# Last layer of a two-layer gated block: the feed-forward's hidden values scaled one batch later, engines' orders rewritten, one reciprocal moved to VectorE

## The chip, the cores and the metric

One core of one Trainium2 chip runs the whole program. The time is the device time of one execution in microseconds (us), and the time shown for a kernel is the median of several executions. One execution was also recorded by the hardware profiler. TensorE is PE in the rows (its weight loads are PEld), VectorE is DVE, ScalarE is ACT, GpSimd is POOL, and SyncE (SP) issues the transfers.

## The reference

`x` and `ctx` are 32 batches of 256 tokens with 256 values each. Two layers are applied; the change touches only the last part of the second one.

```python
x = x + tanh(g_xattn[0]) * attention(layernorm(x), ctx, ctx)      # layer 0
x = x + tanh(g_ffn[0])   * L0_ffn(layernorm(x))
x = x + tanh(g_xattn[1]) * align(ctx, layernorm(x))   # layer 1: time warping of ctx to x
x = x + tanh(g_ffn[1])   * L1_ffn(layernorm(x))       # layer 1: feed-forward

def rmsnorm(x):    return x * rsqrt(mean(x * x, -1, keepdims=True) + 1e-5)
def act_quant(x):                                     # per token
    scale = 127 / clip(max(abs(x), -1), 1e-5)
    return clip(round(x * scale), -128, 127) / scale
def bitlinear(x, w, b):  return act_quant(rmsnorm(x)) @ weight_quant(w).T + b
def L1_ffn(x):                                        # 256 -> 1024 -> 256
    h = gelu(bitlinear(x, w1, b1), approximate=False)
    return bitlinear(h, w2, b2)
```

Each token's vector is thus rounded to integers twice: once at width 256 before the first product, and once at width 1024, after gelu, before the second. Both need the token's mean square and its largest absolute value first, and then a factor.

## The kernel before, in words

The program has three stages in a row. The attention stage (with layer 0's feed-forward) ends near 1250 us of the profile. The alignment stage ends near 1672 us. `last_layer_phase` takes the rest. The change lies in this last stage alone.

The last stage works on 32 batches `n`. A batch is two tiles (`t` = 0, 1) of 128 tokens on 128 partitions. For one batch the steps are: `distance` (ACT) and `path_mask` (DVE) build the alignment mask; `expand` (PE, tile `pe_x`) spreads ctx over the tokens; `residual` (DVE) adds it to x, giving `x3`; `stats`, `aggregate`, `centre`, `x_variance`, `x_maxima` (DVE) prepare the layer norm and the first rounding; `factors` (POOL) turns mean squares (`var`) and maxima (`amax`) into `y` = 1/rms, `q0` = 127/largest value, `q` = `q0*y`, and `back`, the factor for scaling back; `scale_x` (DVE, tile `xr`) and `round_x` (ACT, tile `xq`) round; `inverse_parts` (POOL) writes six columns with 1/`q0` in bf16 pieces behind `xq`; `turn_x` (PE, `pt_x`) transposes; `xqT_copy` (ACT) moves the result to SBUF; `hidden` (PE, `ph`, 12 matmuls) is the first product; `gelu` (ACT, `gl`); `squares` (ACT, `sq` and `ssum`) and `h_maxima` (DVE) prepare the second rounding; `factors` again; `scale_h` (DVE, `hr`) and `round_h` (POOL, `hq`) round; `turn_h` (PE, `pt_h`), `hqT_copy` (ACT) and `output` (PE, `po`, 16 matmuls) are the second product; `output` (DVE, `xo`) adds `x3b`, which `bias` (POOL) made from `x3`; SP stores.

The order is written by hand. Each engine has a loop over rounds `k`, from FIRST = -6 to LAST, and in round `k` it does each step for the batch `k` plus a fixed offset. So a batch passes through the stage over some nine rounds, and each engine meets many batches' steps in one round. Every engine runs its list strictly in order; `w(name, count)` is a wait on a semaphore. A step waits for its inputs, and also for its output buffer to be free: `pe_x`, `pt_x`, `pt_h`, `po`, `xr`, `xq`, `xqT` and `x3` exist once, `ph`, `hr` and `hqT` once for each tile `t`. `Chain` orders small dependent instructions on one engine: `link` waits for the instruction at once, `tick` only counts it, and `hold` waits for all counted so far.

`factors` on POOL handles batch `k+2`'s x and batch `k`'s hidden values together, in tensors of four columns, so that `scale_x(k+2)` and `scale_h(k)` follow on DVE in the same round `k`, behind `w("factors", ...)`.

Of the kernel before, what the change touches and what calls it, by code (L numbers as in the profile page):

```python
# [15 lines left out]
P = 128  # L16
# [1388 lines left out]
def last_layer_phase(nc, io, scr, vin, vout, out, o):  # L1405


    with ExitStack() as ctx:
# [3 lines left out]
        def sem(name):  # L1412
# [11 lines left out]
        x3b = [sb(f"x3b{p}", [P, T, D]) for p in range(6)]  # L1424
# [6 lines left out]
        y, tmp = sb("y4", [P, 2 * T]), sb("tmp4", [P, 2 * T])  # L1431
        back = [sb(f"back{p}", [P, 2 * T]) for p in range(4)]
        ws4, powers = sb("ws4", [P, 2 * T]), sb("powers", [P, 2, 2 * T])
        gl = [[sb(f"gl{p}{t}", [P, F]) for t in range(T)] for p in range(2)]
        sq = [sb(f"sq{t}", [P, F]) for t in range(T)]
        ssum = [sb(f"ssum{p}", [P, T]) for p in range(2)]
# [13 lines left out]
                 "ends", "masked", "x3_res", "x_scaled", "h_scaled", "x4_res", "x_max", "h_max", "factors",  # L1450
# [7 lines left out]
        FIRST, LAST = -6, NB + 2  # L1458
# [4 lines left out]
        @block.sync  # L1463
        def _(sp):
            def w(s, count):
                if count > 0:
                    sp.wait_ge(e[s], count)

            def load(n):
                w("expand", n - 2)  # L1470
                sp.dma_start(cx[n % 3][:], io["ctx_1024"][n].rearrange(tok, p=P)).then_inc(cx_in[n % 3], 16)
                w("x3_res", n - 2)
                sp.dma_start(x2[n % 3][:], scr["x2"][n].rearrange(tok, p=P)).then_inc(x2_in[n % 3], 16)

            def store(n):
                w("x4_res", n + 1)
                sp.dma_start(out[n].rearrange(tok, p=P), xo[n % 2][:]).then_inc(o_out[n % 2], 16)

            for k in range(FIRST, LAST):
                if there(k - 2):  # L1480
                    store(k - 2)
                if there(k + 6):
                    load(k + 6)
            for p in range(2):
                sp.wait_ge(o_out[p], 16 * NB // 2)

        @block.tensor
        def _(pe):
            def w(s, count):
                if count > 0:  # L1490
                    pe.wait_ge(e[s], count)

            def expand(n):
# [15 lines left out]
            def hidden(n):  # L1509
                w("xqT_cp", n + 1)  # L1510
                for t in range(T):
                    w("gelu", 2 * (n - 1) + t + 1)
                    for j in range(2):
                        for c in range(C + 1):
                            last = pe.matmul(ph[t][:, 512 * j:512 * j + 512], xqT[:, c, t * P:t * P + P],  # L1515
                                             w1T[:, c, 512 * j:512 * j + 512], start=(c == 0), stop=(c == C))
                    last.then_inc(e["h_mm"], 1)

            def turn_h(n, t):
                w("h_round", 2 * n + t + 1), w("hqT_cp", 2 * n + t)  # L1520
                for f in range(FT):
                    last = pe.transpose(pt_h[:, f, :], hq[n % 2][t][:, f * P:f * P + P], identb[:])  # L1522
                last.then_inc(e["hq_t"], 1)

            def output(n):
                w("x4_res", n)
                for t in range(T):
                    w("hqT_cp", 2 * n + t + 1)
                    for f in range(FT):
                        last = pe.matmul(po[:, t, :], hqT[t][:, f, :], w2T[:, f, :], start=(f == 0), stop=(f == FT - 1))  # L1530
                last.then_inc(e["o_mm"], 1)

            for k in range(FIRST, LAST):
                if there(k + 1):
                    hidden(k + 1)
                if there(k - 1):
                    turn_h(k - 1, 0)
                if there(k + 4):
                    expand(k + 4)
                if there(k - 1):  # L1540
                    turn_h(k - 1, 1)
                    output(k - 1)
                if there(k + 2):
                    turn_x(k + 2)

        @block.scalar
        def _(act):
# [4 lines left out]
            def gelu(n, t):  # L1552
                w("h_mm", 2 * n + t + 1), w("h_scaled", 2 * (n - 2) + t + 1)
                act.activation(gl[n % 2][t][:], ph[t][:], ACT.Gelu, scale=back[(n - 2) % 4][:, t:t + 1])\  # L1554
                    .then_inc(e["gelu"], 1)

            def squares(n, t):

                w("gelu", 2 * n + t + 1), w("squares", 2 * (n - 1) + t + 1)
                w("h_scaled", 2 * (n - 1))  # L1560
                act.activation(sq[t][:], gl[n % 2][t][:], ACT.Square, accum_out=ssum[n % 2][:, t:t + 1])\  # L1561
# [21 lines left out]
            for k in range(FIRST, LAST):  # L1583
                if there(k):
                    squares(k, 1)
                if there(k + 6):
                    distance(k + 6)
                if there(k - 1):
                    hqT_copy(k - 1, 0)
                if there(k + 1):  # L1590
                    gelu(k + 1, 0)
                if there(k - 1):
                    hqT_copy(k - 1, 1)
                if there(k + 1):
                    gelu(k + 1, 1)
                if there(k + 2):
                    round_x(k + 2)
                if there(k + 1):
                    squares(k + 1, 0)
                if there(k + 2):  # L1600
                    xqT_copy(k + 2)

        @block.gpsimd
        def _(pool):
# [6 lines left out]
            def bias(n):  # L1611
                w("x3_res", n + 1), w("x4_res", n - 5)
                for t in range(T):
                    last = pool.tensor_tensor(x3b[n % 6][:, t, :], x3[:, t, :], b2[:], ALU.add)  # L1614
                last.then_inc(e["x3_bias"], 1)

            def inverse_parts(n):

                w("xq_t", n)
# [13 lines left out]
            def factors(nx, nh):  # L1633
                p = nh % 2
                c = slice(0 if there(nx) else T, 2 * T if there(nh) else T)
                yy, aa = y[:, c], tmp[:, c]
                if there(nh):
                    w("squares", 2 * (nh + 1))
                    pc.link(pool.tensor_scalar(var[p][:, T:2 * T], ssum[p][:], 1.0 / F, EPS, ALU.mult, ALU.add))
# [3 lines left out]
                pc.link(pool.tensor_tensor(yy, var[p][:, c], powers[:, 0, c], ALU.pow))  # L1643
# [9 lines left out]
            pc.tick(pool.memset(powers[:, 0, :], -0.5))  # L1653
            pc.tick(pool.memset(powers[:, 1, :], -1.0))
# [15 lines left out]
        def _(v):  # L1670
# [41 lines left out]
            def h_maxima(n):  # L1712
                for t in range(T):
                    w("gelu", 2 * n + t + 1)
                    last = v.tensor_reduce(amax[n % 2][:, T + t:T + t + 1], gl[n % 2][t][:], AX.X, ALU.max,
# [3 lines left out]
            def output(n, t):  # L1719
                w("x3_bias", n + 1), w("o_mm", n + 1)  # L1720
                if n >= 2:
                    v.wait_ge(o_out[n % 2], 16 * (n // 2))
                ins = v.scalar_tensor_tensor(xo[n % 2][:, t, :], po[:, t, :], back[n % 4][:, T + t:T + t + 1],
                                             x3b[n % 6][:, t, :], ALU.mult, ALU.add)
# [9 lines left out]
            def scale_h(n):  # L1734
                for t in range(T):
                    w("h_round", 2 * (n - 1) + t + 1)
                    v.tensor_scalar(hr_[t][:], gl[n % 2][t][:], q[n % 2][:, T + t:T + t + 1], MAGIC, ALU.mult, ALU.add)\
                        .then_inc(e["h_scaled"], 1)

            def iteration(k):  # L1740
                nx, nh, nr, no, nm = k + 2, k, k + 3, k - 2, k + 5
                isx, ish, isr, iso, ism = (there(n) for n in (nx, nh, nr, no, nm))
                if ish:
                    h_maxima(nh)
                if isr:
                    residual(nr)
                if iso:
                    output(no, 0)
                    output(no, 1)
                if ism:  # L1750
                    path_mask(nm, 0)
                if isr:
                    stats(nr, 0)
                    stats(nr, 1)
                if ism:
                    path_mask(nm, 1)
                if isr:
                    aggregate(nr)
# [3 lines left out]
                    x_variance(nr)  # L1762
                    x_maxima(nr)
                if isx or ish:
                    w("factors", k + 3)
                if isx:
                    scale_x(nx)
                if ish:
                    scale_h(nh)
# [60 lines left out]
```

## Time and profile before

| | us |
|---|---|
| median of 3 executions | 2029.74 (2028.59 to 2030.02) |
| profiled execution | 2029.69 |
| its span | 2027.8 |

| busy in the span | PE | PEld | DVE | ACT | POOL |
|---|---|---|---|---|---|
| us | 1477.6 | 1064.4 | 1526.7 | 1089.5 | 608.0 |

The span covers the instructions of the execution; what lies around it is 1.9 us. The last stage begins at about 1672 us and ends with the span. In its rows an engine's instructions overlap a little: the next one starts some 0.1 us before the end of the one in front, so the time that an instruction holds its engine is read from one start to the next. `[1.18 <-POOL q L1650]` behind a row means that the engine had stood idle for 1.18 us before it, until POOL's instruction of line 1650 released it.

### The profile page before, as it was taken

The page shows a single profiled execution, that of the slowest core. Times are in us where ns is not written, and L with a number is a line of the kernel's source. Part 1 is how long each engine was busy: PE and PEld are TensorE (multiplying, and loading weights), DVE is VectorE, ACT ScalarE, POOL GpSimd, SP SyncE. Part 2 cuts the span into 40 slices and gives each one's busy share as a digit, 9 for nine tenths or more (in the row PEclk, how much of TensorE's full clock was granted, in tenths as well). Part 3 has the DMA queues.
Part 4 walks back from the last instruction along what each step waited for, and adds up shares of the span by engine and source line. Part 5 has one row for each costly group of instructions (what it writes and reads, how often), then busy time and mean ns, then how long its engine had stood idle before and what let it go on. Part 6 is the DMA issues. An engine that isn't in the chain of part 4 may idle for free. (4 is left out here: it accounts for less than half of the span.)

```text
span 2027.8 us, 35980 instructions
## 1 busy us (share of the span) xinstructions
PE 1477.6 (73%) x10790; PEld 1064.4 (52%) x10821; DVE 1526.7 (75%) x4466; ACT 1089.5 (54%) x2304; POOL 608.0 (30%) x1033
## 2 busy tenths in 40 slices
PE   1689999999999999999999986131331007777776
PEld 1467777777777777777777764000000004555554
DVE  7567777777776777777677743799998997888885
ACT  0266666666666666656666562242331005788876
POOL 3111222222222222222222111205000006888886
PEclk9799999999999999999999997555555557999999
DMA  2444443344444434444343310321220003222220
GB/s 79 121 121 132 118 128 111 108 125 112 133 117 115 120 108 129 112 133 113 109 123 105 107 38 18 90 58 39 60 45 7 0 0 99 79 71 78 79 67 32
DMA packets 322938, 179.51 MB, mean 89 GB/s; under 512 B 93793, under 2 KB 318193, under 8 KB 322802
## 3 DMA queue, kind: packets, MB, share of 16 engines
q1 hardware_dynamic: 322802, 178.07, 31.4%
q8 instruction: 40, 0.66, 0.1%
q14 instruction: 96, 0.79, 0.1%
HBM read 122.91 MB, written 50.33 MB: 85 GB/s over the span
## 5 line engine op out<-in xcount | busy, mean ns | idle before, releaser
L805 DVE TENSOR_REDUCE nmax<-s 128x2 f32<-128x512 f32 x512 | 325.4, 682 | 42.3 <-PE s L386 41.0
L601 ACT ACTIVATE pt<-s 128x512 f32<-128x512 f32 x512 | 277.3, 597 | 84.4 <-PE s L401 84.4
L892 POOL TENSOR_TENSOR r<-rl 128x512 f32<-128x512 f32 x128 | 133.1, 1040 | 372.6 <-ACT rl L631 370.0
L386 PE MATMUL s<-kst,qst 96*128 96x256 bf16 x1024 | 164.0, 276 | 19.4 <-DVE nmax L805 12.7
L401 PE MATMUL s<-qst,kst 128*128 128x256 bf16 x1024 | 168.0, 276 | 9.1 <-ACT pt L601 1.4
L1285 PE MATMUL gate<-diag,one 128*128 128x512 f16 x35 | 21.2, 607 | 194.3 <-DVE left L1372 194.3
L631 ACT ACTIVATE rl<-wb,fscl 128x256 f32<-128x256 f32 x256 | 107.3, 472 | 81.9 <-PE wb L483 81.9
L479 PE MATMUL wb<-x2l,wfcT 128*128 128x256 f32 x512 | 143.3, 302 | 0.5 <-ACT dd L651 0.5
L413 PE MATMUL oacc<-pt,vw 128*32 128x256 f32 x2048 | 137.9, 387 | 1.9 <-ACT pt L601 1.9
L350 PE MATMUL wb<-wprT,r2l 128*128 128x256 f32 x512 | 131.1, 295 | 6.9 <-DVE r2l L774 6.9
L480 PE MATMUL wb<-x2h,wfcT 128*128 128x256 f32 x512 | 132.6, 281 | 0.0
L1395 DVE SCALAR_TENSOR_TENSOR hop<-iota,path,steps 32x256 f32<-32x256 f32 x255 | 120.8, 474 | 12.4 <-DMA steps<-step 3.4
L1515 PE MATMUL ph<-w1T,xqT 128*128 128x512 bf16 x353 | 95.8, 428 | 46.9 <-ACT xqT L1576 45.8
L351 PE MATMUL wb<-wprT,r2h 128*128 128x256 f32 x512 | 125.5, 283 | 0.0
L774 DVE TENSOR_TENSOR r2l<-r,r2h 128x512 fp32r<-128x512 f32 x128 | 88.3, 690 | 45.5 <-POOL r L892 45.4
L898 POOL TENSOR_TENSOR half<-ln_mv,ln_y 128x2 f32<-128x2 f32 x32 | 9.3, 292 | 369.0 <-DVE yn L731 369.0
L401 PEld LDWEIGHTS s<-qst,kst 128*128 128x128 bf16 x1024 | 81.4, 98 | 73.2 <-ACT pt L601 48.2
L386 PEld LDWEIGHTS s<-kst,qst 96*128 96x128 bf16 x1024 | 91.4, 98 | 54.1 <-DVE nmax L805 31.9
L1285 PEld LDWEIGHTS gate<-diag,one 128*128 128x128 f16 x35 | 3.6, 104 | 211.6 <-DVE left L1372 193.2
L1359 DVE TENSOR_TENSOR_SCAN rows_r<-best,rows_r,rows_d 128x64 f32<-128x64 f32 x280 | 108.4, 387 | 0.1
L1580 ACT ACTIVATE hqT<-pt_h 128x1024 bf16<-128x1024 bf16 x64 | 65.5, 1023 | 72.5 <-PE pt_h L1522 72.5
L350 PEld LDWEIGHTS wb<-wprT,r2l 128*128 128x128 f32 x512 | 98.7, 193 | 8.6 <-DVE r2l L774 7.9
(265 smaller groups left out, 4079.5 us busy)
## 6 DMA issues: line engine op xcount, KB each, us to landing
kst<-k_parts_dram SPq DMA_DIRECT2D x384, 64.0 KB, 2.6
qst<-q_parts_dram SPq DMA_DIRECT2D x384, 64.0 KB, 2.4
k_parts_dram<-kp SPq DMA_DIRECT2D x32, 384.0 KB, 5.3
q_parts_dram<-qp SPq DMA_DIRECT2D x32, 384.0 KB, 3.1
xin<-in_x_dram SPq DMA_DIRECT2D x32, 256.0 KB, 2.9
cT<-in_ctx_T_dram SPq DMA_DIRECT2D x32, 256.0 KB, 2.7
xres<-in_x_dram SPq DMA_DIRECT2D x32, 256.0 KB, 3.1
cin<-in_ctx_dram SPq DMA_DIRECT2D x32, 256.0 KB, 4.6
```

Source lines behind the costliest of these rows:

```text
L350: pe.matmul(B_PROJ[:, t, :], r2l[:, f, t * P:t * P + P], wprT[:, f, :], start=(f == 0), stop=False)
L351: last = pe.matmul(B_PROJ[:, t, :], r2h[:, f, t * P:t * P + P], wprT[:, f, :], start=False, stop=(f == FT - 1))
L386: last = pe.matmul(s1[h % 2][:, t, :], qst[b.p][0:MAXROW, h, t * P:t * P + P], kst[b.p][0:MAXROW, h, :], start=True, stop=True)
L401: last = pe.matmul(s2[h % 2][:, t, :], kst[b.p][:, h, t * P:t * P + P], qst[b.p][:, h, :], start=True, stop=True)
L413: last = pe.matmul(oacc[HW * j:HW * j + HW, g % 2, :], vw[b.p][:, t, HPG * g + j, :], pt[(HPG * g + j) % (2 * HPG)][:, t, :], start=(t == ...
L479: pe.matmul(B_FC[k][:, j, :], wfcT[:, c, f * P:f * P + P], x2l[:, c, :], start=(c == 0), stop=False)
L480: pe.matmul(B_FC[k][:, j, :], wfcT[:, c, f * P:f * P + P], x2h[:, c, :], start=False, stop=False)
L601: act.activation(pt[h % (2 * HPG)][:], s2[h % 2][:], ACT.Exp).then_inc(e["expd"], 1)
L805: v.tensor_reduce(nmax[:, T * h:T * h + T], s1[h % 2][:], AX.X, ALU.max, negate=True)\
L892: pool.tensor_tensor(r2[:], rl[:, k % 2], rl[:, k % 2], ALU.mult)\
L1359: row = v.tensor_tensor_scan(cost[p][:, i, 1:BW + 1], best[:, i, :], d[:, i, :], cost[p][:, i, 0:1], ALU.min, ALU.add)
L1395: ch.link(v.scalar_tensor_tensor(hop[:], iota[:], path[:, i + 1:i + 2], steps[:, i, :], ALU.is_le, ALU.mult, accum_out=path[:, i:i + 1]))
```

## The change

Of the hidden values' second half of the way, everything from the factor on is moved one round back: `factors` for batch `k-1` instead of `k`, `scale_h` and `round_h` for `k-1`, `turn_h`, `hqT_copy` and PE's `output` for `k-2` instead of `k-1`, DVE's `output` and the store for `k-3` instead of `k-2`. There is one more round (LAST). `gl` and `ssum` get three buffers instead of two, `x3b` eight instead of six, `y` and `tmp` two instead of one.

POOL's `factors` is split. `bounds` stays on POOL, without the two last computations; they go to a new `factors` on DVE: `q0` by the reciprocal instruction, and `q`. POOL's `bias` goes ahead of `inverse_parts`, which now waits for DVE's reciprocal.

```diff
             for k in range(FIRST, LAST):                      # PE
+                if there(k - 2):
+                    turn_h(k - 2, 0)
                 if there(k + 1):
-                    hidden(k + 1)
-                if there(k - 1):
-                    turn_h(k - 1, 0)
+                    turn_x(k + 1)
                 if there(k + 4):
                     expand(k + 4)
-                if there(k - 1):
-                    turn_h(k - 1, 1)
-                    output(k - 1)
-                if there(k + 2):
-                    turn_x(k + 2)
+                if there(k - 2):
+                    turn_h(k - 2, 1)
+                if there(k + 1):
+                    hidden(k + 1, 0)
+                    hidden(k + 1, 1)
+                if there(k - 2):
+                    output(k - 2)
...
             for k in range(FIRST, LAST):                      # ACT
+                    round_x(k + 1)
+                    hqT_copy(k - 2, 0)
+                    xqT_copy(k + 1)
+                    squares(k, 0)
                     squares(k, 1)
                     distance(k + 6)
-                    hqT_copy(k - 1, 0)
+                    hqT_copy(k - 2, 1)
                     gelu(k + 1, 0)
-                    hqT_copy(k - 1, 1)
                     gelu(k + 1, 1)
-                    round_x(k + 2)
-                    squares(k + 1, 0)
-                    xqT_copy(k + 2)
...
-            def factors(nx, nh):                              # POOL
-                p = nh % 2
+            def bounds(k):
+                nx, nh, p = k + 2, k - 1, k % 2
...
                 pc.link(pool.tensor_scalar(aa, aa, 1e-5, 1.0 / 127, ALU.max, ALU.mult))
-                pc.tick(pool.tensor_tensor(q0[p][:, c], aa, powers[:, 1, c], ALU.pow))
                 w("gelu", 2 * (nx - 3)), w("x4_res", nh - 3)
-                pc.link(pool.tensor_tensor(back[nh % 4][:, c], aa, ws4[:, c], ALU.mult))
-                w("x_scaled", nx - 1), w("h_scaled", 2 * (nh - 1))
-                pool.tensor_tensor(q[p][:, c], q0[p][:, c], yy, ALU.mult).then_inc(e["factors"], 1)
+                pool.tensor_tensor(back[k % 4][:, c], aa, ws4[:, c], ALU.mult).then_inc(e["bounded"], 1)
...
-                if there(k + 2) or there(k):
-                    factors(k + 2, k)
+                if there(k + 2) or there(k - 1):
+                    bounds(k)
+                if there(k + 3):
+                    bias(k + 3)
                 if there(k + 2):
                     inverse_parts(k + 2)
-                if there(k + 3):
-                    bias(k + 3)
-                if there(k):
-                    round_h(k, 0)
-                    round_h(k, 1)
+                if there(k - 1):
+                    round_h(k - 1, 0)
+                    round_h(k - 1, 1)
...
+            def factors(k):                                   # DVE
+                w("bounded", k + 3), w("inv_parts", min(k + 1, NB))
+                ce.link(v.reciprocal(q0[p][:, c], tmp[p][:, c]))
+                v.sem_inc(e["factors"], 1)
+                ce.tick(v.tensor_tensor(q[p][:, c], q0[p][:, c], y[p][:, c], ALU.mult))
```

VectorE's list is shown as it stands in the built programs. Before, one round in the middle of the stage reads as follows (`x` is `residual`, `xo` the output, `st` and `mv` the statistics, the first `amax` that of x, the last one that of the hidden values).

```order
L1689 SCALAR_TENSOR_TENSOR x<-pe_x,gates,x_1 128x512
L1723 SCALAR_TENSOR_TENSOR xo<-po,back,x3b 128x256 x2
L1682 TENSOR_SCALAR mask<-apart,reach 128x256
L1694 BN_STATS st<-x 128x6 x2
L1682 TENSOR_SCALAR mask<-apart,reach 128x256
L1699 BN_AGGR mv<-st 128x2 x2
L1702 TENSOR_SCALAR xc<-x,mv 128x256 x2
L1705 TENSOR_SCALAR var_1<-mv 128x2
L1709 TENSOR_REDUCE amax_1<-xc 128x2
L1731 TENSOR_SCALAR xr<-xc,q_0 128x256 x2
L1737 TENSOR_SCALAR hr<-gl,q_0 128x1024 x2
L1715 TENSOR_REDUCE amax_1<-gl 128x1 x2
```

And the same engine and place in the changed program.

```order
L1683 SCALAR_TENSOR_TENSOR x<-pe_x,gates,x_1 128x512
L1688 BN_STATS st<-x 128x6 x2
L1676 TENSOR_SCALAR mask<-apart,reach 128x256
L1693 BN_AGGR mv<-st 128x2 x2
L1676 TENSOR_SCALAR mask<-apart,reach 128x256
L1696 TENSOR_SCALAR xc<-x,mv 128x256 x2
L1699 TENSOR_SCALAR var_0<-mv 128x2
L1709 TENSOR_REDUCE amax_0<-gl 128x1 x2
L1738 RECIPROCAL q_1<-tmp_1 128x4
L1740 TENSOR_TENSOR q_1<-q_1,y_1 128x4
L1703 TENSOR_REDUCE amax_0<-xc 128x2
L1717 SCALAR_TENSOR_TENSOR xo<-po,back,x3b 128x256 x2
```

The maxima of the hidden values, the two factor instructions and the output now stand between the statistics and the scaling (`xr` and `hr`, which follow as before).

TensorE's list before, for one round (`pt_x` is `turn_x`, `ph` `hidden`, `pt_h` `turn_h`, `pe_x` `expand`, `po` `output`).

```order
L1506 MATMUL pt_x<-identb,xq 128x128 x6
L1515 MATMUL ph<-w1T,xqT 128x512 x12
L1522 MATMUL pt_h<-identb,hq 128x128 x8
L1498 MATMUL pe_x<-cx,mask 128x256 x4
L1522 MATMUL pt_h<-identb,hq 128x128 x8
L1530 MATMUL po<-w2T,hqT 128x256 x16
```

And in the changed program.

```order
L1520 MATMUL pt_h<-identb,hq 128x128 x8
L1506 MATMUL pt_x<-identb,xq 128x128 x6
L1498 MATMUL pe_x<-cx,mask 128x256 x4
L1520 MATMUL pt_h<-identb,hq 128x128 x8
L1513 MATMUL ph<-w1T,xqT 128x512 x12
L1528 MATMUL po<-w2T,hqT 128x256 x16
```

`turn_x` no longer stands directly in front of `hidden`: `expand` and a `turn_h` lie between them, and `hidden` is followed at once by `output`.

## Rows read from the trace of the kernel before

**Rows 1.** Busy time of each engine in a stretch of 230 us.

```profile
1750.00:1980.00 230.00, 180.81 (x1276) 121.11 (x1300) 193.02 (x431) 179.97 (x266) 197.71 (x386) 0.96 0.24 75
```

The columns are PE, PEld, DVE, ACT, POOL (busy us and count), granted clock, DMA share, GB/s.

**Rows 2.** Waits, 1750 to 1980 us: in total, times, longest us.

```profile
ACT hqT L1580 <- PE pt_h L1522: 50.0, 45, 4.0
PE ph L1515 <- ACT xqT L1576: 34.4, 23, 1.6
DVE xr L1731 <- POOL q L1650: 28.3, 23, 1.8
POOL var L1639 <- ACT sq L1561: 12.0, 17, 1.9
DVE amax L1715 <- ACT gl L1554: 6.9, 10, 1.0
```

**Rows 3.** Timeline of DVE, 1821 to 1839 us: start, duration, instruction, idle before.

```profile
1821.16 0.74 DVE L1689 SCALAR_TENSOR_TENSOR x<-pe_x,gates,x 128x512 f32<-128x512 f32 x1
1821.82 0.87 DVE L1723 SCALAR_TENSOR_TENSOR xo<-po,back,x3b 128x256 f32<-128x256 f32 x2
1822.60 0.34 DVE L1682 TENSOR_SCALAR mask<-apart,reach 128x256 f32<-128x256 f32 x1
1822.86 0.75 DVE L1694 BATCH_NORM_STATS2 st<-x 128x6 f32<-128x256 f32 x2
1823.53 0.34 DVE L1682 TENSOR_SCALAR mask<-apart,reach 128x256 f32<-128x256 f32 x1
...
1828.83 2.34 DVE L1715 TENSOR_REDUCE amax<-gl 128x1 f32<-128x1024 f32 x2
...
1832.52 0.62 DVE L1682 TENSOR_SCALAR mask<-apart,reach 128x256 f32<-128x256 f32 x1
1833.06 0.74 DVE L1694 BATCH_NORM_STATS2 st<-x 128x6 f32<-128x256 f32 x2
...
1836.84 0.62 DVE L1731 TENSOR_SCALAR xr<-xc,q 128x256 f32<-128x256 f32 x2 [1.18 <-POOL q L1650]
1837.38 1.41 DVE L1737 TENSOR_SCALAR hr<-gl,q 128x1024 f32<-128x1024 f32 x2
1838.70 2.34 DVE L1715 TENSOR_REDUCE amax<-gl 128x1 f32<-128x1024 f32 x2
```

**Rows 4.** Timeline of POOL in the same stretch.

```profile
1830.94 2.05 POOL L1630 TENSOR_SCALAR hq<-hr 128x1024 bf16<-128x1024 f32 x2
1833.18 0.19 POOL L1639 TENSOR_SCALAR var<-ssum 128x2 f32<-128x2 f32 x1 [0.18 <-ACT sq L1561]
...
1835.33 1.03 POOL L1646 TENSOR_TENSOR q<-tmp,powers 128x4 f32<-128x4 f32 x1
1836.34 0.20 POOL L1648 TENSOR_TENSOR back<-tmp,ws 128x4 f32<-128x4 f32 x1
```

**Rows 5.** Small DVE instructions: a group of the attention stage, one of the timeline.

```profile
L812 DVE RECIPROCAL rs<-wb 128x16 f32<-128x16 f32 x64 | 16.2, 253 | 5.1 <-PE wb L427 4.9
```

```profile
1673.04 0.22 DVE L1772 TENSOR_TENSOR reach<-vin,vout 128x64 f32<-128x64 f32 x1
```

**Rows 6.** Timeline of PE: the first product of two neighbouring batches.

```profile
1811.21 4.04 PE L1515 MATMUL ph<-w1T,xqT 128*128 128x512 bf16 x11 [1.63 <-ACT xqT L1576]
...
1822.53 2.54 PE L1515 MATMUL ph<-w1T,xqT 128*128 128x512 bf16 x11 [1.45 <-ACT xqT L1576]
```

**Rows 7.** Timeline of DVE and POOL near the end of the program.

```profile
2017.25 1.42 DVE L1737 TENSOR_SCALAR hr<-gl,q 128x1024 f32<-128x1024 f32 x2 [2.94 <-POOL q L1650]
2018.10 2.48 POOL L1630 TENSOR_SCALAR hq<-hr 128x1024 bf16<-128x1024 f32 x2 [0.88 <-DVE hr L1737]
```

**Rows 8.** Timeline of DVE: the residuals of batches 3, 5 and 31.

```profile
1697.12 0.74 DVE L1689 SCALAR_TENSOR_TENSOR x<-pe_x,gates,x 128x512 f32<-128x512 f32 x1
...
1718.08 0.74 DVE L1689 SCALAR_TENSOR_TENSOR x<-pe_x,gates,x 128x512 f32<-128x512 f32 x1
...
1984.93 0.74 DVE L1689 SCALAR_TENSOR_TENSOR x<-pe_x,gates,x 128x512 f32<-128x512 f32 x1
```

More of the change, by code:

```diff
@@ L1423, in last_layer_phase @@
         x3 = sb("x3", [P, T, D])
-        x3b = [sb(f"x3b{p}", [P, T, D]) for p in range(6)]
+        x3b = [sb(f"x3b{p}", [P, T, D]) for p in range(8)]
         xc, xr = [sb(f"xc{p}", [P, T, D]) for p in range(2)], sb("xr", [P, T, D])
@@ L1430, in last_layer_phase @@
         var, amax, q0, q = ([sb(f"{n}_{p}", [P, 2 * T]) for p in range(2)] for n in ("var4", "amax4", "q0", "q4"))
-        y, tmp = sb("y4", [P, 2 * T]), sb("tmp4", [P, 2 * T])
+        y, tmp = ([sb(f"{n}_{p}", [P, 2 * T]) for p in range(2)] for n in ("y4", "tmp4"))
         back = [sb(f"back{p}", [P, 2 * T]) for p in range(4)]
-        ws4, powers = sb("ws4", [P, 2 * T]), sb("powers", [P, 2, 2 * T])
-        gl = [[sb(f"gl{p}{t}", [P, F]) for t in range(T)] for p in range(2)]
+        ws4, powers = sb("ws4", [P, 2 * T]), sb("powers", [P, 2 * T])
+        gl = [[sb(f"gl{p}{t}", [P, F]) for t in range(T)] for p in range(3)]
         sq = [sb(f"sq{t}", [P, F]) for t in range(T)]
-        ssum = [sb(f"ssum{p}", [P, T]) for p in range(2)]
+        ssum = [sb(f"ssum{p}", [P, T]) for p in range(3)]
         hr_ = [sb(f"hr{t}", [P, F]) for t in range(T)]
@@ L1449, in last_layer_phase @@
                  "xqT_cp", "gelu", "squares", "hqT_cp", "x_round", "distance",
-                 "ends", "masked", "x3_res", "x_scaled", "h_scaled", "x4_res", "x_max", "h_max", "factors",
+                 "ends", "masked", "x3_res", "x_scaled", "h_scaled", "x4_res", "x_max", "h_max", "bounded", "factors",
                  "x3_bias", "h_round", "inv_parts", "centre3", "pool_chain3"]
@@ L1507, in turn_x, with hidden @@
                 last.then_inc(e["xq_t"], 1)
[L1509 to L1517, printed above, removed]
+            def hidden(n, t):
+                w("xqT_cp", n + 1), w("gelu", 2 * (n - 1) + t + 1)
+                for j in range(2):
+                    for c in range(C + 1):
+                        last = pe.matmul(ph[t][:, 512 * j:512 * j + 512], xqT[:, c, t * P:t * P + P],
+                                         w1T[:, c, 512 * j:512 * j + 512], start=(c == 0), stop=(c == C))
+                last.then_inc(e["h_mm"], 1)
             def turn_h(n, t):
@@ L1611, in bias @@
             def bias(n):
-                w("x3_res", n + 1), w("x4_res", n - 5)
+                w("x3_res", n + 1), w("x4_res", n - 7)
                 for t in range(T):
-                    last = pool.tensor_tensor(x3b[n % 6][:, t, :], x3[:, t, :], b2[:], ALU.add)
+                    last = pool.tensor_tensor(x3b[n % 8][:, t, :], x3[:, t, :], b2[:], ALU.add)
                 last.then_inc(e["x3_bias"], 1)
             def inverse_parts(n):
-                w("xq_t", n)
+                w("xq_t", n), w("factors", n + 1)
                 hi, mid_, lo = xq[:, :, D:D + 3], xq[:, :, D + 3:D + 5], xq[:, :, D + 5]
@@ L1714, in h_maxima @@
                     w("gelu", 2 * n + t + 1)
-                    last = v.tensor_reduce(amax[n % 2][:, T + t:T + t + 1], gl[n % 2][t][:], AX.X, ALU.max,
+                    last = v.tensor_reduce(amax[(n + 1) % 2][:, T + t:T + t + 1], gl[n % 3][t][:], AX.X, ALU.max,
                                            apply_absolute_value=True)
@@ L1762, in iteration @@
                     x_variance(nr)
-                    x_maxima(nr)
-                if isx or ish:
-                    w("factors", k + 3)
+                if ish:
+                    h_maxima(nh)
+                if isx or iss:
+                    factors(k)
+                if isr:
+                    x_maxima(nr)
+                if iso:
+                    output(no, 0)
+                    output(no, 1)
+                if isx or iss:
+                    ce.hold()
                 if isx:
                     scale_x(nx)
-                if ish:
-                    scale_h(nh)
+                if iss:
+                    scale_h(ns)
             ce.tick(v.tensor_tensor(mid[:], vin[:], vout[:], ALU.add))
```

56 lines of the change are left out of this document (25 added, 31 removed).

## The prediction

> **What bounds the kernel now.** I read four views in this order. The busy times of a long stretch in the last stage come first [rows 1]: no engine is full. In 230 us, POOL is busy for 197.7, DVE for 193.0, PE for 180.8 and ACT for 180.0 us, and PE's granted clock is 0.96 of full. So some loop of waits between engines sets the pace. The waits of that stretch [rows 2] name it: ACT stands for PE's transposes of the rounded hidden values (50.0 us), PE stands for ACT's copy of the rounded x (34.4 us), and DVE stands for POOL's factors (28.3 us). Everybody waits for somebody.
>
> The timelines then give the pace. Batch 5's residual starts at 1718.08 and batch 31's at 1984.93 [rows 8], so a round takes 266.85 / 26 = 10.26 us. An undisturbed round is 1838.70 - 1828.83 = 9.87 us [rows 3]; the rest comes from some rounds in which the first product takes 4.04 instead of 2.54 us [rows 6], with PE at the lower level of its clock (1.2 instead of 2.4 GHz). Such a round is longer as a whole, which shows that PE lies on the loop.
>
> Two loops are nearly equally long. One is PE and ACT: the copy `xqT` holds up `ph`, `ph`, `pt_h` and `pe_x` stand in front of the second `pt_h`, and ACT's copy of that stands in front of the second gelu, the next `round_x` and so the next `xqT`. The other is POOL alone: in the undisturbed round it idles for 0.18 us only [rows 4]. DVE has most room: it idles for 1.18 of 9.87 us.
>
> **The change, part by part.** I ask of each engine how much it has to do in a round, and then whether a loop across engines is longer.
>
> *POOL.* It loses the power instruction for `q0`: from 1835.33 to 1836.34, 1.01 us [rows 4], and the product for `q`, about 0.25. Its round falls from 9.69 (9.87 - 0.18) to about 8.4 us. It gains a wait for DVE's reciprocal, with `inverse_parts` and `round_h` queued behind it.
>
> *PE and ACT.* Their work stays: per round (10.26 us, so 22.4 rounds in the stretch) 180.8 / 22.4 = 8.07 and 8.03 us [rows 1]; both are upper bounds, since instructions overlap in the rows. The new order takes the loop apart. ACT copies `hqT` while PE transposes x; PE expands while ACT copies `xqT`; and the transposes read values rounded a round earlier, so no step needs a result of the same moment. The first `pt_h` of a round can start when the first `hq` is ready (1.0 us after DVE's residual, worked out below), and the single `po`, last in PE's list, is freed by DVE's output (at about 7.4, in front of `xr` and `hr`). Between the two PE has 6.4 us for the three quarters of its 8.07 us that are not `po`. So the loop of PE and ACT is about 8.1 us, some 1.1 us short of the round forecast here, and each of the two waits about that long in it; a stretch at 1.2 GHz (1.5 us) mostly vanishes in this room and the next round's.
>
> *DVE.* Its round before is 9.87 - 1.18 = 8.69 us. In it the first mask holds the engine from 1832.52 to 1833.06, 0.54 us, where the mask of the round before took 0.26 (1822.60 to 1822.86) [rows 3]; without this hold the round is 8.41. Added are the reciprocal and the product. A DVE product of 64 columns takes 0.22 us, a reciprocal of 16 columns 0.253 [rows 5]; I take 0.22 for each, as both wait for their forerunner, and subtract 0.09, since x's variance no longer needs its own wait. 8.41 + 0.44 - 0.09 = 8.76 us. Bounds for the pair: 0.3 and 0.6.
>
> *DVE against POOL.* Why was that mask long? POOL's two roundings `hq` ran from 1830.94 to 1832.99 [rows 4], and the mask ended at 1833.14, 0.15 us behind them; with POOL idle it took 0.34 us. So such a DVE instruction waits until POOL's instruction is through. The other way round, the two `hq` near the end, beside `hr` on DVE, took 2.48 instead of 2.05 us [rows 7]. In the changed order `hq` always runs right behind the first `hr`: it starts 0.85 us after `hr` and ends 0.85 + 2.48 = 3.33 after it [rows 7]. The first `hq`, with half the stretch, is ready 0.85 + 1.45 = 2.3 after `hr`, that is 1.0 after the next residual. That residual starts 1.32 us after `hr` (1837.38 to 1838.70), the first mask 0.66 + 0.67 = 1.33 after that (residual and statistics, [rows 3]), and would end at 1.67. POOL holds it until 3.33 - 1.32 + 0.15 = 2.16. That is 0.49 us more in every round: 8.76 + 0.49 = 9.25 us. Bounds: 0 (POOL's pieces fall otherwise) and 1.0.
>
> The Trainium skill ("GPSIMD Engine Reference", Key points) says that GpSimd shares its SBUF interfaces with VectorE and contends with VectorE instructions in a 2-port mode or with two SBUF inputs. The mask rows agree with its first half. By its second half the new product for `q` (two SBUF inputs) could be held as well, for which the trace of before has no row; that is taken up as a rival.
>
> *Does DVE wait for POOL?* POOL's bounds start when `hq` ends, at 2.0, and last from 1833.18 to 1836.54 less the 1.01 removed, 2.4 us [rows 4]: ready at 4.4. DVE asks when all but the last 0.44 + 0.6 + 0.78 + 0.54 + 1.32 of its 9.25 us is done (factors, x's maximum, output, `xr`, `hr`), at 5.6. 1.2 us spare. The closed loop reciprocal, output, `xr`, `hr`, `hq`, bounds is 0.4 + 0.6 + 0.8 + 0.5 + 3.3 + 2.4 = 8.0 us, under 9.25. So DVE's own work is the new bound, and its lists hold no wait.
>
> *Start of the stage.* Before, the residuals of batches 3 and 5 lie 20.96 us apart [rows 8], for two rounds in which everybody waits for factors and first products. Now DVE carries no output in these two rounds and no `hr` in the first: 9.25 - 0.78 - 0.49 - 1.32 = 6.7 and 9.25 - 0.78 = 8.5 (its own hold is small here), less 0.5, 14.7 us together. Batch 3's residual comes some 2.5 us earlier, since `expand` no longer stands behind the first `ph`. Batch 5's residual: 1697.1 - 2.5 + 14.7 = 1709.3. Bounds: 1706 and 1718.
>
> *End.* From batch 31's residual to the end of the span it is now 2027.8 - 1984.9 = 42.9 us. Then: the last scaling but four begins 7.7 us after that residual; each later one follows at `hq` 3.33, bounds 1.9 (two columns) or 2.4, reciprocal and product 0.44, output 0.88, in all 6.6 (7.4 for the first, with `xr`); four of them make 7.7 + 7.4 + 3 x 6.6 = 34.9. From the last `hr` it is 2027.8 - 2017.25 = 10.55 as now. Together 45.4, that is 2.5 more for the additional round. Bounds: 42 and 52.
>
> *Sum.* 1709.3 + 8.5 (round 2, without output) + 25 x 9.25 = 1949.0 for batch 31's residual, + 45.4 = 1994.4, + 1.9 around the span = 1996.3. The profiled execution had 2029.69, the median is 2029.74, so I say 1996 us, 34 less: 27 from the rounds, 9 from the start, less 2.5 at the end.
>
> **Rivals.**
>
> A, no hold: if POOL's roundings don't reach the mask, a round is 8.76 to 8.85 and the time 25 x 0.45 = 11 less: 1985 us. For it: in the round of 1822.60 the mask was free; against: POOL's order now ties `hq` to `hr`.
>
> B, more contention: the product for `q` is held by POOL's `bias` (two instructions of 0.7 us, which end near 5.9, where DVE asks for the product), and `inverse_parts` and `xr` hold each other up. Price 0.3 to 0.75 us in a round, 10.0 us at the most: 2004 to 2015 us. For it: the rows of the mask; against: in my schedule `bias` has just ended.
>
> C, the change doesn't do what it says: the loop of PE and ACT stays at 9.87 and its disturbed rounds too. 25 x 0.8 = 20 more: about 2016, only start and POOL being better. Against: every PE step's input is older than before.
>
> D, slower: PE at 1.2 GHz through the stage. PE's round of about 7.7 us at 2.4 GHz would be near 14 (the first product alone 4.0 and more), above all others, and the time some 30 x 4 = 120 us above now. It decides once more than 0.4 of the stage lies at the lower level, because 7.7 + 0.4 x 6.6 passes 10.3 (7.7 is what the 8.07 leave without the present stretches at 1.2 GHz). For it: the level fell in rounds where PE had idled for 1.6 us before `ph`; against: the granted clock is 0.96 over 230 us [rows 1], and PE will idle less than before, not more.
>
> The Trainium skill ("TensorE: Matmul & The Clock Gate", The HAM clock gate) ties the clock to how busy the array has been. By that rule a shorter round at equal work keeps it high, which is against D.
>
> **Chances.** Forecast 0.70, A 0.08, B 0.10, C 0.07, D 0.05. The range: the forecast's own bounds are 1986 to 2008 (round 8.9 to 9.7, start and end by their bounds); taking in A's edge and most of B, 1985 to 2013 leaves out C, D and part of B, less than 0.2. A change within 0.2% (4 us, what a measurement can tell) would need a round of 10.5 us and lies beyond C: 0.03. Faster 0.92, slower 0.05.
>
> **What would show it.** Right: DVE without idle time in the middle, rounds of 9.2 to 9.3 us, the first mask at about 0.8 us behind `hq`, PE waiting for DVE's output before `po`, ACT waiting about 1 us for `pt_h`, and no long rounds where `ph` takes 4 us. Wrong: DVE idle before the reciprocal (POOL too late), before the hidden maxima (gelu too late), a product for `q` of over 0.4 us, or batch 5's residual later than 1718.

## The result, and the profile after

The changed kernel takes 1992.21 us (median of 4, 1991.38 to 1992.80) against 2029.16 us for the kernel before on the same chip. The ratio is 0.982, with a 95% interval of 0.980 to 0.984: 37 us faster, where 34 were forecast and 1996 us named. The profiled execution had 1992.80 us with a span of 1991.0 us.

VectorE's timeline of one round in the middle (start, duration, instruction) answers to [rows 3].

```profile
1836.28 0.74 DVE L1683 SCALAR_TENSOR_TENSOR x<-pe_x,gates,x 128x512 f32<-128x512 f32 x1
1837.06 0.75 DVE L1688 BATCH_NORM_STATS2 st<-x 128x6 f32<-128x256 f32 x2
1837.73 0.69 DVE L1676 TENSOR_SCALAR mask<-apart,reach 128x256 f32<-128x256 f32 x1
1838.35 0.23 DVE L1693 BATCH_NORM_AGGREGATE mv<-st 128x2 f32<-128x6 f32 x2
1838.50 0.32 DVE L1676 TENSOR_SCALAR mask<-apart,reach 128x256 f32<-128x256 f32 x1
...
1839.33 2.33 DVE L1709 TENSOR_REDUCE amax<-gl 128x1 f32<-128x1024 f32 x2
1841.59 0.16 DVE L1738 RECIPROCAL q<-tmp 128x4 f32<-128x4 f32 x1
1841.89 0.16 DVE L1740 TENSOR_TENSOR q<-q,y 128x4 f32<-128x4 f32 x1
1842.09 0.69 DVE L1703 TENSOR_REDUCE amax<-xc 128x2 f32<-128x512 f32 x1
...
1845.33 0.74 DVE L1683 SCALAR_TENSOR_TENSOR x<-pe_x,gates,x 128x512 f32<-128x512 f32 x1
```

No row has an idle time behind it, and the next residual comes after 1845.33 - 1836.28 = 9.05 us. The reciprocal and the product hold the engine from 1841.59 to 1842.09, 0.50 us. The first mask holds it for 0.62 us (1837.73 to 1838.35), where a free one takes 0.26.

POOL's timeline of the same round answers to [rows 4]. Its two `hq` wait for `hr`, start while it still runs, take 2.48 us together (as in [rows 7]) and end at 1838.28. The mask ends 0.14 us behind them.

```profile
1835.80 2.48 POOL L1628 TENSOR_SCALAR hq<-hr 128x1024 bf16<-128x1024 f32 x2 [1.20 <-DVE hr L1731]
1838.36 0.19 POOL L1637 TENSOR_SCALAR var<-ssum 128x2 f32<-128x2 f32 x1
```

The waits of 1750 to 1940 us (total, times, longest) answer to [rows 2]. DVE is never the engine that waits. Everybody waits for DVE or for what hangs on it.

```profile
POOL hq L1628 <- DVE hr L1731: 25.2, 21, 1.2
PEld pt_h L1520 <- POOL hq L1628: 23.3, 21, 1.1
ACT hqT L1580 <- PE pt_h L1520: 22.0, 21, 1.8
PEld po L1528 <- DVE xo L1717: 21.2, 21, 1.0
PE po L1528 <- DVE xo L1717: 10.8, 21, 0.5
```

Busy times of that stretch (columns as in [rows 1]) show DVE at 185.4 of 190 us, and PE's granted clock at 1.00.

```profile
1750.00:1940.00 190.00, 161.71 (x1221) 111.09 (x1219) 185.44 (x441) 167.97 (x251) 148.44 (x316) 1.00 0.27 86
```

The residuals of batches 5 and 31 answer to [rows 8].

```profile
1710.47 0.74 DVE L1683 SCALAR_TENSOR_TENSOR x<-pe_x,gates,x 128x512 f32<-128x512 f32 x1
...
1944.74 0.75 DVE L1683 SCALAR_TENSOR_TENSOR x<-pe_x,gates,x 128x512 f32<-128x512 f32 x1
```

So the gain is 7.6 us at the start (1718.08 - 1710.47), 32.6 in the 26 rounds between (266.85 - 234.27), and 3.4 are given back at the end (46.3 instead of 42.9). About a third of the 32.6 comes from PE's slow stretches, which are gone: before, seven rounds between the two residuals were some 1.5 us longer than the others, because the first product ran at the lower clock.

### The profile page after: what moved, and what is told of

It is laid out like the page before. It is cut to its first block and busy times, and to the rows that moved or that the text cites. A ratio compares the mean times of both kernels' runs of the same rounds, so it can differ in the third digit from the quotient of the medians.

```text
span 1991.0 us, 36114 instructions
## 1 busy us (share of the span) xinstructions
PE 1468.9 (74%) x10821; PEld 1063.7 (53%) x10821; DVE 1537.1 (77%) x4536; ACT 1087.6 (55%) x2304; POOL 557.1 (28%) x968
## 5 line engine op out<-in xcount | busy, mean ns | idle before, releaser
L1567 ACT ACTIVATE apart<-iota,mid 128x256 f32<-128x256 f32 x64 | 28.4, 499 | 135.8 <-DVEq L1781 131.1
L351 PEld LDWEIGHTS wb<-wprT,r2h 128*128 128x128 f32 x512 | 99.0, 193 | 0.0
```

Of the source, the lines that this page charges most:

```text
L351: last = pe.matmul(B_PROJ[:, t, :], r2h[:, f, t * P:t * P + P], wprT[:, f, :], start=False, stop=(f == FT - 1))
```

## The experiments

Each kernel ran on the same chip as the kernel before; ratios are to it, with 95% intervals. The changed kernel has 0.982. Where times of two runs are set against each other, the kernel before took 2028.3 to 2029.9 us on the chips concerned. The code cuts show the main lines of each edit. Where an edit only moves steps, the cut shows the engine's list of steps in words instead of code.

**One part alone: the reciprocal** (in the kernel before)

```diff
-                pc.tick(pool.tensor_tensor(q0[p][:, c], aa, powers[:, 1, c], ALU.pow))
...
-                pool.tensor_tensor(q[p][:, c], q0[p][:, c], yy, ALU.mult).then_inc(e["factors"], 1)
...
+                    ce.link(v.reciprocal(q0[p][:, c], tmp[p][:, c]))
+                    v.sem_inc(e["factors"], 1)
+                    ce.link(v.tensor_tensor(q[p][:, c], q0[p][:, c], y[p][:, c], ALU.mult))
```

> The kernel before with only the reciprocal and the product for q moved to DVE; no delay, no new orders. My theory (the loop of PE and ACT at 9.81 us is closed by the order of their lists, POOL at 9.69 is only second): the same time as before within 3 us, 2026 to 2032, the long rounds with ph at 4 us stay. Rival (POOL's factors are what the loop waits for): the round falls by about 0.5 us, 2014 or less.

Measured: 2028.51 us, ratio 0.9996 (0.9987 to 1.0005). No change. PE's timeline keeps the round of 9.81 us and the long rounds (the third row below is a slow first product):

```profile
1839.40 2.77 PE L1515 MATMUL ph<-w1T,xqT 128*128 128x512 bf16 x12 [1.23 <-ACT xqT L1576]
1849.21 2.76 PE L1515 MATMUL ph<-w1T,xqT 128*128 128x512 bf16 x12 [1.23 <-ACT xqT L1576]
1859.03 4.45 PE L1515 MATMUL ph<-w1T,xqT 128*128 128x512 bf16 x12 [1.23 <-ACT xqT L1576]
```

POOL now waits 34.7 us for ACT's squares in 230 us: it has the time that it was given and no use for it. So POOL's own work was not the bound. PE still stands for ACT's `xqT` for 1.23 us in every round.

**The delay without the orders of PE and ACT** (in the changed kernel)

```diff
-  PE:  turn_h(k-2,0) turn_x(k+1) expand turn_h(k-2,1) hidden(k+1) output(k-2)
+  PE:  hidden(k+1) turn_h(k-2,0) expand turn_h(k-2,1) output(k-2) turn_x(k+2)
-  ACT: round_x(k+1) hqT(k-2,0) xqT(k+1) squares(k,0) squares(k,1) distance hqT(k-2,1) gelu gelu
+  ACT: squares(k,1) distance hqT(k-2,0) gelu hqT(k-2,1) gelu round_x(k+2) squares(k+1,0) xqT(k+2)
```

> The changed kernel, hidden values scaled one batch later and reciprocal on DVE, but PE and ACT run their steps in the relative order of before (ph, pt_h, pe_x, pt_h, po, pt_x; gelu between the two hqT copies, round_x and xqT behind). Theory 1 (the orders break the loop): the chain xqT, ph, pt_h, pe_x, pt_h, hqT, gelu, round_x, xqT stays, round 9.8 us plus long rounds, 2020 to 2034 us. Theory 2 (the delay breaks it, the orders hardly matter): DVE's 9.04 us round stays, 1990 to 1998 us.

Measured: 2029.89 us, ratio 1.0004 (0.9995 to 1.0013). All other edits together bring nothing while PE and ACT keep their order. The first products again follow each other by 9.82 us, each with the wait for `xqT`, and every fourth one is slow again (4.45 us at 1866.12). So the lists of PE and ACT close the loop. Which of the two lists would have sufficed was not tested.

```profile
1846.48 2.76 PE L1513 MATMUL ph<-w1T,xqT 128*128 128x512 bf16 x12 [1.23 <-ACT xqT L1575]
1856.30 2.76 PE L1513 MATMUL ph<-w1T,xqT 128*128 128x512 bf16 x12 [1.23 <-ACT xqT L1575]
```

**The orders without the delay** (batch `k`'s hidden values are scaled in round `k`)

```diff
-                nx, nh, p = k + 2, k - 1, k % 2
+                nx, nh, p = k + 2, k, k % 2
...
-                nx, nh, nr, no, nm, ns = k + 2, k, k + 3, k - 3, k + 5, k - 1
+                nx, nh, nr, no, nm, ns = k + 2, k, k + 3, k - 2, k + 5, k
```

> The changed kernel without the delay: new orders on PE, ACT, POOL and DVE, reciprocal on DVE, but the hidden values of batch k (not k-1) are scaled and rounded in round k. Theory: the new orders need the delay, because squares of batch k now come behind hqT and xqT in round k, and the scaling waits for them. Loop: hqT 0.9, xqT 0.7, squares 2.1, bounds 2.4, factors 0.5, maximum 0.6, output 0.8, xr 0.5, hr and first hq 2.3, pt_h 0.5 = 11.3 us a round, about 1.1 longer than before: 2040 to 2065 us. Rival: the orders alone bring the gain, 1990 to 2000 us.

Measured: 2088.93 us, ratio 1.030 (1.028 to 1.032), 24 us above the expected range. The chain of waits is the one named:

```profile
POOL var L1637 <- ACT sq L1561: 65.2, 17, 4.2
PEld po L1528 <- DVE xo L1717: 61.4, 17, 4.1
PE po L1528 <- DVE xo L1717: 53.0, 17, 3.6
DVE q L1738 <- POOL back L1645: 46.0, 17, 3.2
```

POOL waits for the squares, DVE for POOL, PE for DVE. The mean round is 12.04 us (24 rounds from 1735.65 to 2024.52), not 11.3. At full clock it is 11.76 (residuals at 1790.83 and 1802.59), so the sum of the expectation was 0.5 us short. The rest is PE's clock, granted at 0.91: in about every second round PE is at the lower level behind its wait of 3.2 us, `pt_h` on the loop takes 1.04 instead of 0.62 us, and the round is 12.16 us (1778.67 to 1790.83).

```profile
1779.71 1.04 PE L1520 MATMUL pt_h<-identb,hq 128*128 128x128 bf16 x8
1791.88 0.62 PE L1520 MATMUL pt_h<-identb,hq 128*128 128x128 bf16 x8 [0.83 <-POOL hq L1628]
```

So, with the reciprocal moved, neither the orders nor the delay suffice alone. This run keeps the new lists of DVE and POOL as well; the new lists of PE and ACT alone, without the delay, were not run.

**The undo of the reciprocal** (in the changed kernel)

```diff
-                ce.link(v.reciprocal(q0[p][:, c], tmp[p][:, c]))
-                v.sem_inc(e["factors"], 1)
-                ce.tick(v.tensor_tensor(q[p][:, c], q0[p][:, c], y[p][:, c], ALU.mult))
...
+                pc.link(pool.tensor_tensor(q0[p][:, c], aa, powers[:, 1, c], ALU.pow))
...
+                pool.tensor_tensor(q[p][:, c], q0[p][:, c], yy, ALU.mult).then_inc(e["bounded"], 1)
```

> The changed kernel with the last two factor instructions back on POOL (power for q0, product for q), so that DVE has neither; order and delay stay. My theory (DVE's own list is the bound of the changed kernel, POOL close behind): DVE's round falls from 9.04 to about 8.6 us, POOL's grows from 7.84 (9.04 less 1.20 idle) by 1.03 + 0.08 + 0.27 to 9.2, so POOL takes over with little loss: round 9.2 to 9.4, 1996 to 2003 us. Rival (the reciprocal on VectorE brought most of the gain): 2010 us or more.

Measured: 2015.82 us, ratio 0.993 (0.992 to 0.995). That is 13 us above my range, and the rival's number was right: worth nothing in the old order, moving the two factor instructions is worth 24 us in the new one. POOL's timeline shows why:

```profile
1844.75 1.41 POOL L1612 TENSOR_TENSOR x3b<-x,b 128x256 f32<-128x256 f32 x2
1846.14 0.46 POOL L1619 TENSOR_SCALAR inv<-q,wback 128x2 f32<-128x2 f32 x1
1846.67 0.21 POOL L1620 CAST xq<-inv 128x6 bf16<-128x6 f32 x1
1846.96 0.58 POOL L1621 TENSOR_TENSOR rest<-inv,xq 128x2 f32<-128x2 f32 x1
1847.61 0.60 POOL L1622 CAST xq<-rest 128x4 bf16<-128x4 f32 x1
...
1848.82 2.08 POOL L1628 TENSOR_SCALAR hq<-hr 128x1024 bf16<-128x1024 f32 x2
```

`inverse_parts` comes later and meets DVE's `xr` and `hr`: pieces of 0.2 us take 0.6. POOL has no idle time left, and its round is 9.79 us (the `hq` before this one starts at 1839.03). I had taken `inverse_parts` at its undisturbed length.

**More work on VectorE**

```diff
+                    for j in range(2):
+                        ce.link(v.tensor_reduce(spare[:, j:j + 1], iota[:], AX.X, ALU.max))
```

> The changed kernel with two additional small reductions (128x256 fp32, some 0.37 us each with their waits, result unused) on DVE in each of 35 rounds, between output and xr. If DVE's own list is the bound, the round grows by the whole of it, 0.7 to 0.8 us, to about 9.8 us, and the time by about 29 x 0.75 = 22 us, to 2010 to 2018; if another loop is the bound, under 8 us more. It also makes PE idle as long in a round as before (some 2.1 us): if it is PE's idle time that brings its clock down to 1.2 GHz, long first products of 4 us come back; if not, none.

Measured: 2022.92 us, ratio 0.997 (0.996 to 0.998): 30.7 us more than the changed kernel, and 5 above the expected range. The two reductions hold DVE for 0.90 us, not 0.75:

```profile
1840.07 0.86 DVE L1772 TENSOR_REDUCE spare<-iota 128x1 f32<-128x256 f32 x2
1840.97 0.62 DVE L1726 TENSOR_SCALAR xr<-xc,q 128x256 f32<-128x256 f32 x2
```

The round is 9.945 us, exactly 0.90 more than 9.045. Between the residuals of batches 5 and 31 (1714.33 and 1972.06) that makes 23.5 us; the start takes 3.9 more and the end 3.7. DVE's list is the bound.

**More work on TensorE**

```diff
+                for c in range(2):
+                    pe.matmul(ph[t][:, 0:512], xqT[:, c, t * P:t * P + P], w1T[:, c, 0:512], start=True, stop=True)
```

> The changed kernel with four additional matmuls (128x512 bf16) on PE in each batch, in front of the real ones of the first product, which overwrite them: 4 x 0.215 = 0.86 us more PE work in a round. In the changed kernel PE idles 0.52 us in front of po and 0.83 us in front of the first pt_h, 1.35 us in all. If DVE's list is the bound, the round stays at 9.04 us and the time within 2 us of 1992; if PE is on the bounding loop, about 29 x 0.86 = 25 us more.

Measured: 1993.84 us, ratio 0.982 (0.981 to 0.984), as the changed kernel. The 0.86 us disappear in PE's waits; PE is not on the loop.

**VectorE's old order** (in the changed kernel)

```diff
-  residual, statistics, mask 0, aggregate, mask 1, centre, x_variance, h_maxima, factors, x_maxima, output
+  h_maxima, residual, output, mask 0, statistics, mask 1, aggregate, centre, x_variance, x_maxima, factors
```

> The changed kernel (delay, orders of PE and ACT, POOL's list, reciprocal on DVE) with DVE's list in the order of before: hidden maxima first, output before the masks, x's maximum before the factors. POOL's hq then falls beside the hidden maxima, which it does not hold, so the mask is free (0.49 us less), but inverse_parts falls beside xr and hr and is stretched again. DVE's list: 8.41 + 0.5 = 8.9 us, POOL's closed loop 8.4 to 8.8. If DVE's order mattered only through the hold: round 8.9 to 9.0, 1987 to 1993 us. If the new DVE order was itself needed to break a loop: a round of 9.4 us or more, 2003 us or more.

Measured: 2012.12 us, ratio 0.992 (0.990 to 0.993). Round 9.67 us. The number is in the range of the expectation's second case, but its reason is not in the rows: DVE has no idle time there, so no other loop had closed. The first mask is free, but another hold appears that I hadn't seen coming: `xc` takes 1.44 instead of 0.60 us, beside POOL's `bias` (1842.64, 1.46 us).

```profile
1842.81 1.44 DVE L1696 TENSOR_SCALAR xc<-x,mv 128x256 f32<-128x256 f32 x2
```

That makes 0.84 us of hold in place of 0.36, most of the 0.63 by which the round is longer. The rest is about what the new list had gained by putting independent instructions next to each other (worked out below).

**The hidden maxima early** (in the changed kernel, VectorE's list)

```diff
-  residual, statistics, mask 0, aggregate, mask 1, centre, x_variance, h_maxima, reciprocal, product, x_maxima
+  residual, statistics, h_maxima, mask 0, aggregate, mask 1, centre, x_variance, reciprocal, x_maxima, product
```

> The changed kernel with the hidden maxima directly behind the statistics (beside POOL's hq, which does not hold a reduction) and the masks behind them; and with the product for q behind x's maximum, so that it does not meet POOL's bias. If the hold of the first mask is paid for in full by the round (theory: DVE's list is the bound): 9.04 - 0.38 = 8.66 us in a round, about 1980 to 1984 us. If something else is as long as 9.0 us: within 3 us of 1992.

Measured: 2004.10 us, ratio 0.988 (0.986 to 0.990), in neither of the expected ranges. Again slower than the changed kernel, and again by `bias`: the mask takes 0.34 us, but `xc` and x's variance now lie beside `bias` (1847.12, 1.57 us).

```profile
1847.02 1.09 DVE L1696 TENSOR_SCALAR xc<-x,mv 128x256 f32<-128x256 f32 x2
1848.03 0.69 DVE L1699 TENSOR_SCALAR var<-mv 128x2 f32<-128x2 f32 x1
```

Even an instruction on two columns (0.16 us by itself) waited 0.5 us.

**POOL's `bias` first** (in the kernel just above)

```diff
-  POOL: bounds(k) bias(k + 3) inverse_parts(k + 2)      DVE: reciprocal, x_maxima, product
+  POOL: bias(k + 3) bounds(k) inverse_parts(k + 2)      DVE: x_maxima, reciprocal, product
```

> As the last run with early hidden maxima, but POOL's bias (two instructions of 0.7 us) stands in front of its bounds, right behind hq, where DVE is still in the hidden maxima, and DVE takes x's maximum before the reciprocal. If it was the bias that held xc and x's variance in that run (0.47 and 0.5 us in a round of 9.57), and in the run with DVE's old order (0.8 us), the holds go and the round is 8.6 to 8.8 us: 1980 to 1987 us. If such holds come from any POOL instruction, the power instruction of bounds, which now lies beside the masks and xc, holds these instead: 9.3 us or more, 1998 us or more.

Measured: 1994.51 us, ratio 0.983 (0.982 to 0.984), between the two expected ranges. All holds on DVE are gone (`xc` 0.61, variance 0.16 us), so it was the `bias`, not any POOL instruction; the power of `bounds` (1842.08, 1.28 us) beside the second mask and `xc` holds nothing. But the round is 9.04 us once more, now with DVE idle before the reciprocal:

```profile
1844.30 0.18 DVE L1738 RECIPROCAL q<-tmp 128x4 f32<-128x4 f32 x1 [0.19 <-POOL back L1645]
```

`bounds` behind `bias` comes too late, and POOL's loop (bounds, reciprocal, stretched `inverse_parts`, `hq`, `bias`) is the bound: POOL idles only for 0.45 us in the round, for the reciprocal. That its length is that of the changed kernel's round I take for chance.

**VectorE's list fitted to POOL's** (the changed kernel's POOL list; DVE as follows)

```diff
+  residual, statistics, hidden maxima of tile 0, mask 0, aggregate, mask 1, centre, x_variance,
+  hidden maxima of tile 1, reciprocal, x_maxima, product for q, output, scale_x, scale_h
```

> The changed kernel with POOL's list as it is and DVE's list fitted to it: the first tile's hidden maxima stand behind the statistics (POOL's hq ends beside them), then masks, xc and x's variance (beside POOL's small instructions and its power), then the second tile's maxima (beside POOL's bias), the reciprocal, x's maximum and then the product for q. So no DVE instruction that hq or bias held in the other runs lies beside them. Theory (holds by POOL's long instructions are the last 0.4 us of the changed kernel's round, DVE's list is the bound): 8.6 to 8.7 us a round, 1979 to 1984 us. Rival (another loop of 9.0 us lies right below, as POOL's did in the run with bias first): 1990 to 1995 us.

Measured: 1982.57 us, ratio 0.977 (0.975 to 0.978), as expected: 47 us faster than before and 10 faster than the changed kernel. Round 8.57 us, no hold and no idle time:

```profile
1840.70 1.20 DVE L1709 TENSOR_REDUCE amax<-gl 128x1 f32<-128x1024 f32 x1
1841.82 0.35 DVE L1676 TENSOR_SCALAR mask<-apart,reach 128x256 f32<-128x256 f32 x1
...
1842.47 0.61 DVE L1696 TENSOR_SCALAR xc<-x,mv 128x256 f32<-128x256 f32 x2
1842.99 0.17 DVE L1699 TENSOR_SCALAR var<-mv 128x2 f32<-128x2 f32 x1
1843.06 1.22 DVE L1709 TENSOR_REDUCE amax<-gl 128x1 f32<-128x1024 f32 x1
```

## Why the prediction was right, step by step

*The old bound.* "Two loops are nearly equally long", PE and ACT first, POOL second: shown. Relieving POOL alone gave nothing; only the new order of PE and ACT together with the delay gave something. POOL's rank as a close second showed in the new order, where its factor instructions cost 24 us and the round was 9.78 us, next to the 9.81 of before.

*The new bound.* "DVE's own work is the new bound, and its lists hold no wait": shown, by 0.90 us more work that cost 0.90 us a round, and by 0.86 us more on PE that cost nothing. POOL's bounds were ready at 1840.61, 1.0 us before DVE asked for them (1.2 forecast). PE waits 1.34 us in a round and ACT 1.0, where about 1.1 each were forecast.

*DVE's round.* 9.25 us forecast, 9.04 measured. Reciprocal and product: 0.44 less 0.09 forecast, 0.50 measured. Hold of the first mask: 0.49 forecast, 0.36 measured. The mask starts 1.45, not 1.33 us after the residual, because the statistics now follow the residual directly and wait for its end (0.78 instead of 0.66 us), so less of `hq` was left. The remainder, 9.04 - 0.50 - 0.36 = 8.18, is 0.23 under the 8.41 of before: where independent instructions now stand next to each other (variance and maxima 0.07 us apart instead of 0.20, aggregates and mask 0.15 instead of 0.27), waits between dependent ones are hidden. I had counted only 0.09 of that. This term was mis-sized, by about 0.15 us, 4 us in all. The first `hq` took 1.48 us; the forecast's 1.45 was right, but it holds the whole stretch of 0.43 us and not, as it says, half of it.

*POOL's round.* 8.4 us forecast, 7.84 measured (9.04 less 1.20 idle). `inverse_parts` no longer meets `xr` and `hr`, so its pieces take 0.2 instead of 0.6 us. The forecast didn't see this; since POOL was not the bound, the time didn't need it.

*Start and end.* Batch 5's residual at 1709.3 forecast, 1710.5 measured. From batch 31's residual to the end 45.4 forecast, 46.3 measured. The last `hr` begins 34.84 us after that residual, for 34.9 forecast (the 7.4 for the first step, where its own terms with `xr` and the longer bounds give 7.6, was 7.44). The term that was too short is the last, taken "as now": 11.4 us instead of 10.55. The last batch's `pt_h` stands behind a `po` at the lower clock, 3.28 us long instead of 1.92:

```profile
1979.72 3.28 PE L1528 MATMUL po<-w2T,hqT 128*128 128x256 bf16 x16
```

*The total.* It came within 4 us partly by luck: the 26 rounds were 5.5 us shorter than forecast, the start 1.2 and the end 0.9 longer. In the start, batch 3's residual came at 1695.0 (1694.6 forecast), and the two rounds behind it took 15.5 us, not 14.7. In the round, too, errors partly cancel: the hold was put 0.13 us too high and the gain by the new neighbours 0.14 too low, the reciprocal and the product 0.06 too low.

*PE's slow stretches.* I had them vanish in PE's spare time. In fact they don't occur in the middle of the stage: no first product takes 4 us, and the granted clock from 1750 to 1940 us is 1.00.

```profile
1840.35 2.75 PE L1513 MATMUL ph<-w1T,xqT 128*128 128x512 bf16 x12
```

The lower level comes back only at the end (granted clock 0.81 from 1960 to 1991 us). The forecast of the time didn't need the difference, but the reason was wrong. Why they are gone is not shown.

*Rivals.* A: a round of 9.04 lies between forecast and A, but the hold was there, 0.36 us of it. B: its mechanism is real and showed up where the masks are missing, in the last two full rounds. There DVE reaches the product for `q` earlier in the round, while POOL's `bias` runs (1940.04 to 1941.46):

```profile
1940.45 0.17 DVE L1738 RECIPROCAL q<-tmp 128x4 f32<-128x4 f32 x1
1940.76 0.71 DVE L1740 TENSOR_TENSOR q<-q,y 128x4 f32<-128x4 f32 x1
```

It takes 0.71 instead of 0.16 us. The second half of the Trainium skill's rule ("GPSIMD Engine Reference", Key points: contention with VectorE instructions with two SBUF inputs) agrees with these rows, 0.71 against 0.16 us. C is refuted for the whole change, and is what happens when PE and ACT keep their order. Its price was too low, though: by its own words (9.87 and the disturbed rounds) it is 1.0 us a round and not 0.8, and the run with the old order took 2029.9 us, not 2016. There the mean round was 10.06 us, as C had it; the start and the end were longer than it had them. D did not happen: PE's work in a round was 7.70 us (9.04 less 1.34), as forecast for the full clock.

## What to carry to other kernels

A loop that goes through several in-order lists can need edits that work together: here, with the reciprocal moved in each case, the delay without the orders gave 0, the orders without the delay 60 us more, and both 37 us less. Ask of each step where in the round its input becomes ready, and put it behind that on every engine. When one engine's list has become the bound, look in its rows for instructions that take longer than their own kind, see what runs beside them, and move the pair apart; here that gave another 10 us, once both lists were looked at together.

## What the runs showed of the hardware that I had not expected

*Which POOL instructions hold DVE.* `hq` (1024 columns, one input) holds DVE's mask (0.69 us instead of 0.34). `bias` (256 columns, two inputs) holds `xc` (1.44 instead of 0.60), the variance on two columns (0.69 instead of 0.16) and the product for `q` (0.71 instead of 0.16). Each ends just behind the POOL instruction that it met. The power on four columns, which runs for 1.04 us, holds nothing that could be seen. DVE's maxima (2.33 us beside `bias`, as elsewhere), its statistics (0.75 beside `hq`) and the residual, which reads PSUM (0.74 beside `hq`), run freely. The other way round, `xr` and `hr` on DVE stretch POOL's small pieces from 0.2 to 0.6 us and the two `hq` from 2.05 to 2.48.

*PE's clock and idle time.* In the kernel before, PE idles about 2.2 us in a round, its longest wait is 1.6 us, and the lower level comes back about every 41 us, in each fourth round (first products of 4.02 us at 1770.30, of 4.04 at 1811.21 [rows 6], and so on). With the added DVE work PE idles as much, (36.4 + 11.3) us in 21 rounds = 2.3 each (1750 to 1960 us), and no first product is slow from 1702 to 1988 us (one near the end, at 1993.83, takes 4.20):

```profile
PE pt_h L1521 <- POOL hq L1629: 36.4, 21, 1.7
PE po L1529 <- DVE xo L1718: 11.3, 22, 0.5
```

So the amount of idle time in a round does not decide by itself. The two kernels also differ in where it lies (before `ph` there, before `pt_h` here) and in the length of the round (9.82 and 9.945 us), and no run separates these. The Trainium skill ("TensorE: Matmul & The Clock Gate", The HAM clock gate) ties the clock to how busy the array has been; these two kernels are too alike in that to be told apart by it (PE busy for 149.6 and 146.8 of the 190 us from 1750 to 1940). What brings the slow stretches stays open.
